# Phase D of a two-layer decoder: five hand-written engine orders in rounds of slots, with tanh, exponential, sums and moments as pieces of their own

## Chip, cores, metric

One core of one Trainium2 chip. The metric is the device time in microseconds of one launch, the median of the runs. The engines are TensorE (PE), VectorE (DVE), ScalarE (ACT), GpSimd (POOL) and SyncE (SP), which issues most DMAs; each runs its own list of instructions in order, and they meet by semaphores.

## The reference, cut to what matters

A decoder of two layers works on x of 32 × 256 × 256. Each layer has attention, cross attention and a feed-forward part, each behind a layernorm. The change touches only the attention of layer 1, which attends over the batch: for each of the 256 positions its 32 items attend to one another.

```python
def _L1_attn_ref(x, Wq, Wk):
    q = jnp.einsum('sbd,ed->sbe', x, Wq)
    k = jnp.einsum('sbd,ed->sbe', x, Wk)
    scores = jnp.einsum('sbd,tbd->bst', q, k) / scale
    align = jax.nn.softmax(jnp.tanh(scores), axis=2)
    return jnp.einsum('bst,tbd->sbd', align, x)
...
x = x + _L0_ffn_ref(_layernorm(x), ...)
x = x + _L1_attn_ref(_layernorm(x), L1_attn_Wq, L1_attn_Wk)
x = x + _L1_xattn_ref(_layernorm(x), ctx_768, ...)
```

## The kernel before, in words

The kernel has four phases with a barrier of all engines after each: A (layer 0, both attentions and routing), C (the 16 experts), **D** (this attention) and E (the rest of layer 1). Phase D runs from about 1885 to 2062 us of the span.

Phase D has `STEPS_D` = 16 steps. One takes 16 positions of all 32 items, 512 rows of 256 numbers: four groups g of 128 rows (a group is 32 items times 4 positions). For step t:

- SP loads slots, rows and gates (`sp_d_load`, ring of 4), the first four steps in phase C, the others when the sum `x3` of the step four earlier is made.
- POOL gathers each row's expert answer by four indirect DMAs (`pool_d_gather`, L1952, ring of 2).
- DVE adds gate × answer + x into `x3` (L1963), takes statistics (L1968), aggregates (L1972), and adds epsilon to the variance (L1976). POOL raises that to the power −1/2 (L1982). DVE normalises into `xn` (L1990).
- PE turns `xn` in two halves (`pe_d_turn`, L2000); ACT copies each (L2010). PE projects in two halves with the joined weights (`pe_d_project`, L2018); ACT copies each (L2028). PE scores (`pe_d_score`, L2037), all four groups into one bank.
- ACT takes tanh (L2048) and exponential (L2050) of the 128 × 512 scores. DVE masks them, so that a row sees its own position only (L2057).
- PE sums, a group at a time, with a column of ones for the denominator (`pe_d_sum`, L2065), into banks 4 and 5 in turn: sum g waits until out g − 2 has read the bank. DVE takes the reciprocal (L2073) and writes the output rows (L2076). SP stores the step (L2083).

The trace has two records for each matmul of project, score and sum, and one for each of turn.

The order is written out by hand in a loop over rounds for each engine: in round t a piece with lag 3 works on step t − 3. PE: score and then turn, two sums, project, two sums, where turn and project have lag 3 and the others lag 4. DVE: mask (lag 4), add and moments (lag 2), outs 0 and 1 (lag 4), normalise (lag 2), outs 2 and 3 (lag 4). ACT: tanh and exponential (lag 4), both copies of turn, both of project (lag 3). POOL: gather (lag 1), power (lag 2). SP: load (lag 0), store (lag 4).

The other phases are written with a helper that puts each piece at a slot of a round:

```python
def due(n, period, slots, items=B):
    for k, slot in enumerate(slots):
        b, off = divmod(n - slot, period)
        if off == 0 and 0 <= b < items:
            yield b, k
```

The functions that the diff touches, with what calls them:

Of the kernel before, what the change touches and what calls it, by code (L numbers as in the profile page):

```python
# [12 lines left out]
ACT = mybir.ActivationFunctionType  # L13
# [110 lines left out]
def item(t, lag, n=B):  # L124
    return t - lag if 0 <= t - lag < n else None
# [1917 lines left out]
def act_d_exp(c, t):  # L2043
    s, par = c.sa.s, t % 2
    flat = c.sa.weight[par][:, :, :].rearrange("p g n -> p (g n)")
    c.act.wait_ge(s.scored, t + 1)
    c.act.wait_ge(s.summed, 4 * (t - 1))
    c.nc.scalar.activation(flat, c.banks[par][:, :], ACT.Tanh, scale=1.0 / math.sqrt(D)).then_inc(s.exp, 1)  # L2048
    c.act.wait_ge(s.exp, 2 * t + 1)
    c.nc.scalar.activation(flat, flat, ACT.Exp).then_inc(s.exp, 1)  # L2050


def dve_d_mask(c, t):

    s, r, par = c.sa.s, c.sa, t % 2
    c.dve.wait_ge(s.exp, 2 * t + 2)
    c.nc.vector.tensor_tensor(r.weight[par][:, :, :], r.weight[par][:, :, :],  # L2057
                              r.same[:, :].unsqueeze(1).broadcast_to([P, G, P]), ALU.mult).then_inc(s.weight, 1)


def pe_d_sum(c, t, g):
    s, r, bank = c.sa.s, c.sa, 4 + g % 2
    c.pe.wait_ge(s.weight, t + 1)
    c.pe.wait_ge(*c.bank_out[bank])
    c.nc.tensor.matmul(c.banks[bank][:, 0:D + 1], r.weight[t % 2][:, g, :], r.xn[t % 4][:, g, :], start=True,  # L2065
                       stop=True).then_inc(s.summed, 1)
    c.bank_out[bank] = (s.out, 4 * t + g + 1)
# [20 lines left out]
def pe_phase_d(c):  # L2090
    for t in range(LAST_D):
        t3, t4 = (item(t, lag, STEPS_D) for lag in (3, 4))
        if t4 is not None:
            pe_d_score(c, t4)
        if t3 is not None:
            for k in range(KC):
                pe_d_turn(c, t3, k)
        if t4 is not None:
            for g in range(2):
                pe_d_sum(c, t4, g)  # L2100
        if t3 is not None:
            for n in range(KC):
                pe_d_project(c, t3, n)
        if t4 is not None:
            for g in range(2, G):
                pe_d_sum(c, t4, g)


def act_phase_d(c):
    for t in range(LAST_D):  # L2110
        t3, t4 = (item(t, lag, STEPS_D) for lag in (3, 4))
        if t4 is not None:
            act_d_exp(c, t4)
        if t3 is not None:
            for k in range(KC):
                act_d_xn_t(c, t3, k)
            for n in range(KC):
                act_d_project(c, t3, n)


def dve_phase_d(c):
    for t in range(LAST_D):
        t2, t4 = (item(t, lag, STEPS_D) for lag in (2, 4))
        if t4 is not None:
            dve_d_mask(c, t4)
        if t2 is not None:
            dve_d_stats(c, t2)
        if t4 is not None:
            for g in range(2):
                dve_d_out(c, t4, g)  # L2130
        if t2 is not None:
            dve_d_normed(c, t2)
        if t4 is not None:
            for g in range(2, G):
                dve_d_out(c, t4, g)


def pool_phase_d(c, d):
    for t in range(LAST_D):
        t1, t2 = (item(t, lag, STEPS_D) for lag in (1, 2))  # L2140
        if t1 is not None:
            pool_d_gather(c, d["expert_out"], t1)
        if t2 is not None:
            pool_d_power(c, t2)


def sp_phase_d(c, d):
    out_rows = d["x4"].rearrange("b (t q g) d -> t b q g d", g=G, q=Q)
    for t in range(LAST_D):
        t0, t4 = (item(t, lag, STEPS_D) for lag in (0, 4))  # L2150
        if t0 is not None and t0 >= 4:
            sp_d_load(c, d, t0)
        if t4 is not None:
            sp_d_out(c, out_rows[t4], t4)
# [414 lines left out]
```

## Time and profile before

| | |
|---|---|
| median of 3 runs | 3380.1 us (3377.64 to 3380.84) |
| profiled execution | 3377.66 us, its span 3375.9 us |
| granted clock over the span | 0.972 of full speed |
| busy: PE, DVE, ACT, POOL | 92%, 69%, 53%, 38% |

The profile is of one execution. "PE L2018 ... x8" in its timeline is eight records on line 2018, run one after the other; "[1.20 <-DVE sa_p L2057]" says that the engine was idle for 1.20 us before, and what ended that. A group's length there counts to the end of its last record, and where records overlap, the next group starts before that end. The names of tiles are `sa_xn` (normalised rows), `sa_xnt` (turned), `sa_q` (projected), `sa_p` (weights), `sa_rec` (reciprocals), `sa_y` (gathered), `sa_g` (gates).

### The profile page before, as it was taken

To read this page: it belongs to the slowest core of one execution; us is meant where nothing else is said; L and a number is where in the kernel's file an instruction comes from. 1 tells how busy PE (TensorE), PEld (TensorE's weight loads), DVE (VectorE), ACT (ScalarE), POOL (GpSimd) and SP (SyncE) were. 2 spreads that over 40 slices of the span, in tenths; PEclk is the share of its full clock that TensorE was granted. 3 is DMA by queue.
4 is the path that set the end of the run, shared out by engine and by line. 5 is a ranking of instruction groups with operands and counts; after the bars stand their busy time and mean duration, and the time that the engine had idled before them with its cause. 6 is when DMAs were issued, how large, how long until landed. Compare 5 with 4: busy or idle time off the path is not lost. (4 is left out here: it accounts for less than half of the span.)

```text
span 3375.9 us, 57669 instructions
## 1 busy us (share of the span) xinstructions
PE 3101.4 (92%) x21302; PEld 2150.3 (64%) x21302; DVE 2328.1 (69%) x4781; ACT 1799.4 (53%) x3243; POOL 1295.6 (38%) x1933
## 2 busy tenths in 40 slices
PE   3899999999999998699999786899999999999997
PEld 2566666666666665466666453576766667666764
DVE  3588888888888887242111484687888877888774
ACT  3788788888788874211111132555555555555552
POOL 4366666666666663100000351233333333333322
PEclk8899999999999999799999897999999999999998
DMA  5877777878777873333333253433433434433420
GB/s 99 149 119 107 105 109 108 112 101 110 104 107 108 108 99 48 118 117 117 117 104 123 78 168 80 64 62 58 68 60 56 62 59 67 63 56 59 62 39 13
DMA packets 291102, 301.17 MB, mean 89 GB/s; under 512 B 35243, under 2 KB 278427, under 8 KB 290821
## 3 DMA queue, kind: packets, MB, share of 16 engines
q1 hardware_dynamic: 276420, 273.41, 48.4%
q0 software_dynamic: 6144, 15.68, 1.6%
q10 hardware_dynamic: 8256, 8.39, 0.8%
q8 instruction: 169, 2.77, 0.4%
q14 instruction: 113, 0.92, 0.1%
HBM read 95.51 MB, written 50.40 MB: 43 GB/s over the span
## 5 line engine op out<-in xcount | busy, mean ns | idle before, releaser
L493 DVE TENSOR_REDUCE xa_mx<-bank 128x2 f32<-128x512 f32 x1024 | 670.5, 688 | 151.8 <-PE bank L483 146.5
L597 ACT ACTIVATE xa_p<-bank 128x512 f32<-128x512 f32 x1024 | 568.5, 599 | 310.6 <-PE bank L587 305.4
L608 DVE SCALAR_TENSOR_TENSOR xa_p<-xa_p,bank 128x1024 f32<-128x1024 f32 x256 | 306.6, 1217 | 38.4 <-PE bank L576 23.4
L933 POOL TENSOR_SCALAR_AFFINE_SELECT xa_p<-xa_p 128x256 f32<-128x256 f32 x512 | 201.7, 406 | 222.1 <-ACT xa_p L924 209.8
L620 PE MATMUL bank<-xa_p,xa_v 128*32 128x256 f32 x4096 | 277.3, 389 | 1.7 <-DVE xa_p L608 1.4
L924 ACT ACTIVATE xa_p<-bank 128x384 f32<-128x384 f32 x512 | 236.9, 492 | 54.3 <-PE bank L912 36.0
L1952 POOL DMA_INDIRECT sa_y<-expert_out,sa_s x64 | 70.1, 1095 | 508.2 <-POOLq L1853 482.5
L1747 ACT ACTIVATE ex_h<-bank,ex_b 128x512 f32<-128x512 f32 x64 | 44.0, 687 | 361.7 <-PE bank L1736 361.7
L1736 PE MATMUL bank<-ex_xt,ex_w 128*128 128x512 f32 x512 | 224.6, 597 | 0.7 <-ACT ex_xt L1727 0.7
L1766 PE MATMUL bank<-ex_w,ex_h 128*128 128x256 f32 x1024 | 224.0, 379 | 1.0 <-issue 0.9
L587 PE MATMUL bank<-ex_w,xa_ks 99*128 99x256 bf16 x1024 | 183.9, 277 | 30.5 <-ACT xa_p L597 22.2
L1766 PEld LDWEIGHTS bank<-ex_w,ex_h 128*128 128x128 f32 x1024 | 193.4, 190 | 28.1 <-issue 2.4
L587 PE MATMUL bank<-xa_qs,xa_ks 99*128 99x256 bf16 x1024 | 185.2, 279 | 21.8 <-DMA xa_qs<-xa_row 16.2
L483 PE MATMUL bank<-xa_ks,ex_w 96*128 96x256 bf16 x1024 | 189.3, 276 | 16.3 <-DMA ex_w<-xa_pq 9.6
L483 PE MATMUL bank<-xa_ks,xa_qs 96*128 96x256 bf16 x1024 | 181.7, 274 | 5.8 <-DVE xa_mx L493 4.3
L1551 POOL TENSOR_TENSOR fp_v<-fp_v,fp_p 128x1408 f32<-128x1408 f32 x32 | 101.6, 3174 | 214.3 <-DVE fp_v L1542 214.3
L912 PE MATMUL bank<-ex_w 96*128 96x256 f16 (+1 forms) x1024 | 156.2, 250 | 21.4 <-DMA ex_w<-ra_parts 7.9
L2262 PE MATMUL bank<-ff_wg,fe_xnt 128*128 128x352 f32 x512 | 173.9, 463 | 0.9 <-ACT fe_xnt L2255 0.7
L454 PE MATMUL bank<-ff_wd,fe_ht 128*128 128x256 f32 x768 | 172.7, 382 | 0.7 <-ACT fe_ht L1651 0.7
L1736 PEld LDWEIGHTS bank<-ex_xt,ex_w 128*128 128x128 f32 x512 | 98.0, 192 | 118.0 <-issue 116.1
L620 PEld LDWEIGHTS bank<-xa_p,xa_v 128*32 128x32 f32 x4096 | 107.5, 109 | 99.1 <-issue 35.7
L1776 DVE TENSOR_TENSOR ex_y<-bank,ex_b 128x256 f32<-128x256 f32 x64 | 27.2, 425 | 203.6 <-PE bank L1766 203.6
(284 smaller groups left out, 6849.1 us busy)
## 6 DMA issues: line engine op xcount, KB each, us to landing
ex_w<-ra_parts SPq DMA_DIRECT2D x384, 128.0 KB, 6.6
xa_ks<-xa_pk SPq DMA_DIRECT2D x384, 128.0 KB, 4.6
ex_w<-in_L_ffn_W SPq DMA_DIRECT2D x32, 1024.0 KB, 7.2
xa_qs<-xa_pq SPq DMA_DIRECT2D x192, 128.0 KB, 4.7
ex_w<-xa_pq SPq DMA_DIRECT2D x192, 128.0 KB, 4.6
ra_x<-in_x SPq DMA_DIRECT2D x32, 256.0 KB, 8.1
xa_ctx<-in_ctx_t SPq DMA_DIRECT2D x64, 128.0 KB, 3.9
queue<-zeros ACTq DMA_DIRECT2D x4, 2048.0 KB, 7.9
```

What stands on the lines that cost most here:

```text
L454: m = c.nc.tensor.matmul(ps[:, tc * D:(tc + 1) * D], left[:, k, tc * P:(tc + 1) * P], right[:, k, :], start=(k == 0), stop=(k == chunks - 1))
L483: m = c.nc.tensor.matmul(ps[:, tc * S:(tc + 1) * S], c.xa.q_stack[par][0:STACK3, h, tc * P:(tc + 1) * P], c.xa.k_stack[par][0:STACK3, h, : ...
L493: c.nc.vector.tensor_reduce(c.xa.row_max[:, :, n], halves(c.banks[2 + n % 2]), AX.X, ALU.max).then_inc(s.max_taken, 1)
L587: m = c.nc.tensor.matmul(ps[:, kc * S:(kc + 1) * S], c.xa.k_stack[par][:, h, kc * P:(kc + 1) * P], c.xa.q_stack[par][:, h, :], start=True, ...
L597: c.nc.scalar.activation(c.xa.p_beside[:, n // 2 % 4, :, n % 2, :], halves(c.banks[n % 2]), ACT.Exp, scale=SCALE).then_inc(s.exp, 1)
L608: c.nc.vector.scalar_tensor_tensor(out=p, in0=p, scalar=1.0, in1=c.banks[bank][:, :].unsqueeze(1).broadcast_to([P, TC, 2 * S]), op0=ALU.mi ...
L620: m = c.nc.tensor.matmul(bank[WIDE * quad:WIDE * quad + WIDE, at + q0:at + S], v[:, kc, 4 * g + quad, :], p(4 * g + quad, kc), start=(kc = ...
L924: c.nc.scalar.activation(c.xa.p_after[:, n // 2 % 4, n % 2, 0:S + P], c.banks[n % 2][:, 0:S + P], ACT.Exp, scale=1.0 / math.sqrt(2.0 * DH) ...
L933: c.nc.gpsimd.affine_select(out=diagonal, in_=diagonal, compare_op=ALU.is_ge, fill=0.0, base=0, pattern=[[0, TC], [1, P]], channel_multipl ...
L1736: m = c.nc.tensor.matmul(c.banks[bank][:, :], r.w1[par][:, k, m1 * P:(m1 + 1) * P], r.x_t[par][:, k, :], start=(k == 0), stop=(k == KC - 1))
L1766: m = c.nc.tensor.matmul(c.banks[bank][:, 0:D], r.hid[par][:, k, q * P:(q + 1) * P], r.w2[par][:, k, :], start=(k == 0), stop=(k == MC - 1))
L2262: m = c.nc.tensor.matmul(c.banks[bank][:, 0:HALF], c.ff.xn_t[:, k, tc * P:(tc + 1) * P], w[:, k, cols], start=(k == 0), stop=(k == KC - 1))
```

## The change

All five order functions of phase D are written with `due`, each with a period for its engine and a slot for each piece. `act_d_exp` is cut into tanh and exponential with a semaphore each, and `dve_d_stats` into the addition and the moments; each of the four sums and outs has a slot of its own. The bank of the scores is now freed by the tanh's semaphore. The addition has one more wait, for the outs of the step four before. Line numbers in the changed kernel are larger by 7 to 18.

```diff
-    s.scored, s.exp, s.weight = c.sem("sa_score", n), c.sem("sa_exp", 2 * n), c.sem("sa_w", n)
+    s.scored, s.tanh, s.exp, s.weight = (c.sem("sa_" + name, n) for name in ("score", "tanh", "exp", "w"))
...
-def dve_d_stats(c, t):
+def dve_d_add(c, t):
...
     c.dve.wait_ge(s.y_in[par], 64 * (t // 2 + 1))
+    c.dve.wait_ge(s.out, 4 * (t - 3))
     for g in range(G):
         m = dve.scalar_tensor_tensor(out=r.x3[at][:, g, :], in0=r.y[par][:, g, :], scalar=r.gate[at][:, g:g + 1],
                                      in1=r.x[at][:, g, :], op0=ALU.mult, op1=ALU.add)
     m.then_inc(s.x3, 1)
+
+
+def dve_d_moments(c, t):
+    s, r, dve, at = c.sa.s, c.sa, c.nc.vector, t % 4
     c.dve.wait_ge(s.x3, t + 1)
...
-    c.bank_out[bank] = (s.exp, 2 * t + 1)
+    c.bank_out[bank] = (s.tanh, t + 1)
...
+def act_d_tanh(c, t):
     s, par = c.sa.s, t % 2
     c.act.wait_ge(s.scored, t + 1)
     c.act.wait_ge(s.summed, 4 * (t - 1))
-    c.nc.scalar.activation(flat, c.banks[par][:, :], ACT.Tanh, scale=1.0 / math.sqrt(D)).then_inc(s.exp, 1)
-    c.act.wait_ge(s.exp, 2 * t + 1)
-    c.nc.scalar.activation(flat, flat, ACT.Exp).then_inc(s.exp, 1)
+    c.nc.scalar.activation(flat_weight(c, t), c.banks[par][:, :], ACT.Tanh, scale=1.0 / math.sqrt(D)).then_inc(s.tanh, 1)
+
+
+def act_d_exp(c, t):
+    s = c.sa.s
+    c.act.wait_ge(s.tanh, t + 1)
+    c.nc.scalar.activation(flat_weight(c, t), flat_weight(c, t), ACT.Exp).then_inc(s.exp, 1)
...
-LAST_D = STEPS_D + 4
+ROUND_D = dict(pe=9, dve=8, act=6, pool=2, sp=2)
...
 def pe_phase_d(c):
-    for t in range(LAST_D):
...
+    period = ROUND_D["pe"]
+    for n in range((STEPS_D - 1) * period + 48):
+        for b, k in due(n, period, (27, 28), STEPS_D):
+            pe_d_turn(c, b, k)
...
+        for b, k in due(n, period, (41, 42, 44, 47), STEPS_D):
+            pe_d_sum(c, b, k)
```

PE's other slots are 30 and 31 for project and 34 for score. DVE: add 16, moments 18, normalise 20, mask 33, outs 35, 37, 38, 39. ACT: copies of turn 19, 20, copies of project 22, 23, tanh 24, exponential 27. POOL: gather 2, power 5. SP: load 0, store 9.

TensorE in a steady round, before. L2037 is score, L2000 turn, L2065 sum, L2018 project.

```order
L2037 MATMUL bank<-sa_q,sa_xnt 128x128 x8
L2000 MATMUL bank<-ident,sa_xn 128x128 x8
L2065 MATMUL bank<-sa_xn,sa_p 128x257 x2
L2018 MATMUL bank<-sa_xnt,sa_wqk 128x512 x4
L2065 MATMUL bank<-sa_xn,sa_p 128x257 x2
```

And in the changed kernel, from one turn to the next. L2048 is score, L2011 turn, L2083 sum, L2029 project.

```order
L2011 MATMUL bank<-ident,sa_xn 128x128 x8
L2083 MATMUL bank<-sa_xn,sa_p 128x257
L2029 MATMUL bank<-sa_xnt,sa_wqk 128x512 x4
L2083 MATMUL bank<-sa_xn,sa_p 128x257 x2
L2048 MATMUL bank<-sa_q,sa_xnt 128x128 x8
L2083 MATMUL bank<-sa_xn,sa_p 128x257
```

With turn of step u, the row before it is the third sum of u − 2, the one behind it the fourth of u − 2, the two behind project are the first two of u − 1. Before, all four sums of a step stood between its score and the next step's score, the first two behind the next turn; now a step's first sum stands behind the next step's project, and its fourth behind the turn of the step after.

VectorE in a steady round, before, from one mask on (L2057 mask, L1963 add, L1968, L1972 and L1976 moments, L2073 and L2076 outs, L1990 normalise; one more pair of out rows follows).

```order
L2057 TENSOR_TENSOR sa_p<-sa_p,sa_same 128x512
L1963 SCALAR_TENSOR_TENSOR sa_x<-sa_y,sa_g,sa_x 128x256 x4
L1968 BN_STATS sa_stats<-sa_x 128x6 x4
L1972 BN_AGGR sa_mv<-sa_stats 128x2 x4
L1976 TENSOR_SCALAR sa_var<-sa_mv 128x4
L2073 RECIPROCAL sa_rec<-bank 128x1
L2076 SCALAR_TENSOR_TENSOR sa_out<-bank,sa_rec,sa_x 128x256
L2073 RECIPROCAL sa_rec<-bank 128x1
L2076 SCALAR_TENSOR_TENSOR sa_out<-bank,sa_rec,sa_x 128x256
L1990 TENSOR_SCALAR sa_xn<-sa_x,sa_mv,sa_rstd 128x256 x4
L2073 RECIPROCAL sa_rec<-bank 128x1
L2076 SCALAR_TENSOR_TENSOR sa_out<-bank,sa_rec,sa_x 128x256
```

And in the changed kernel, from an add on (L1970 add, L2075 mask, L1979, L1983 and L1987 moments, L2091 and L2094 outs, L2001 normalise; two more pairs of out rows follow).

```order
L1970 SCALAR_TENSOR_TENSOR sa_x<-sa_y,sa_g,sa_x 128x256 x4
L2075 TENSOR_TENSOR sa_p<-sa_p,sa_same 128x512
L1979 BN_STATS sa_stats<-sa_x 128x6 x4
L1983 BN_AGGR sa_mv<-sa_stats 128x2 x4
L1987 TENSOR_SCALAR sa_var<-sa_mv 128x4
L2091 RECIPROCAL sa_rec<-bank 128x1
L2094 SCALAR_TENSOR_TENSOR sa_out<-bank,sa_rec,sa_x 128x256
L2001 TENSOR_SCALAR sa_xn<-sa_x,sa_mv,sa_rstd 128x256 x4
L2091 RECIPROCAL sa_rec<-bank 128x1
L2094 SCALAR_TENSOR_TENSOR sa_out<-bank,sa_rec,sa_x 128x256
```

The add now stands before the mask, one out instead of two between the variance and normalise, and three outs instead of two behind normalise. ScalarE takes the exponential of a step behind the copies of the next step's turn, no longer right behind its tanh. The rows of POOL and SP stand in the order they had.

## Rows read from the trace of the kernel before

**Rows 1.** The page's part 1: busy time, share of the span, instructions, engine by engine

```profile
PE 3101.4 (92%) x21302; PEld 2150.3 (64%) x21302; DVE 2328.1 (69%) x4781; ACT 1799.4 (53%) x3243; POOL 1295.6 (38%) x1933
```

**Rows 2.** Waits from 1909 to 2058: engine, line, waited for: us in total, times, longest

```profile
PE bank L2065 <- DVE sa_p L2057: 20.1, 16, 2.1
```

**Rows 3.** Stretches: us, busy us of each engine, granted clock, DMA share, GB/s

```profile
1937.07:2040.27 103.20, 89.99 (x442) 61.08 (x440) 86.08 (x287) 37.27 (x67) 56.06 (x51) 1.00 0.48 154
2070.00:2100.00 30.00, 16.76 (x56) 9.81 (x57) 10.82 (x23) 4.17 (x7) 4.77 (x5) 0.65 0.55 81
```

**Rows 4.** Timeline of a steady round: start us, us, engine, line, operation, idle before

```profile
1922.07 1.06 ACT L2010 ACTIVATE sa_xnt<-bank 128x512 f32<-128x512 f32 x2
1922.19 0.69 DVE L2057 TENSOR_TENSOR sa_p<-sa_p,sa_same 128x512 f32<-128x512 f32 x1 [1.26 <-ACT sa_p L2050]
...
1922.94 1.14 PE L2065 MATMUL bank<-sa_xn,sa_p 128*128 128x257 f32 x4 [1.20 <-DVE sa_p L2057]
...
1923.91 3.60 PE L2018 MATMUL bank<-sa_xnt,sa_wqk 128*128 128x512 f32 x8
...
1926.36 0.17 DVE L1976 TENSOR_SCALAR sa_var<-sa_mv 128x4 f32<-128x4 f32 x1
...
1926.62 1.04 POOL L1982 TENSOR_TENSOR sa_rstd<-sa_var,mhalf 128x4 f32<-128x4 f32 x1 [2.86 <-DVE sa_var L1976]
...
1927.35 1.12 PE L2065 MATMUL bank<-sa_xn,sa_p 128*128 128x257 f32 x4
1927.55 0.60 ACT L2028 ACTIVATE sa_q<-bank 128x512 f32<-128x512 f32 x1 [1.12 <-PE bank L2018]
1927.69 1.38 DVE L1990 TENSOR_SCALAR sa_xn<-sa_x,sa_mv,sa_rstd 128x256 f32<-128x256 f32 x4
...
1928.31 1.95 PE L2037 MATMUL bank<-sa_q,sa_xnt 128*128 128x128 f32 x16
...
1928.99 0.16 DVE L2073 RECIPROCAL sa_rec<-bank 128x1 f32<-128x1 f32 x1
...
1929.59 0.16 DVE L2073 RECIPROCAL sa_rec<-bank 128x1 f32<-128x1 f32 x1
...
1930.09 1.04 PE L2000 MATMUL bank<-ident,sa_xn 128*128 128x128 f32 x8
...
1930.92 0.63 ACT L2050 ACTIVATE sa_p<-sa_p 128x512 f32<-128x512 f32 x1
```

**Rows 5.** Timeline: normalise and turn of step 0, score of step 0, normalise of step 2

```profile
1897.90 1.44 DVE L1990 TENSOR_SCALAR sa_xn<-sa_x,sa_mv,sa_rstd 128x256 f32<-128x256 f32 x4 [1.17 <-POOL sa_rstd L1982]
...
1899.40 1.97 PE L2000 MATMUL bank<-ident,sa_xn 128*128 128x128 f32 x8 [17.81 <-DVE sa_xn L1990]
...
1909.43 2.05 PE L2037 MATMUL bank<-sa_q,sa_xnt 128*128 128x128 f32 x16 [0.69 <-ACT sa_q L2028]
...
1918.31 1.44 DVE L1990 TENSOR_SCALAR sa_xn<-sa_x,sa_mv,sa_rstd 128x256 f32<-128x256 f32 x4
```

**Rows 6.** Timeline of the phase's end: the last four sums, reciprocals and outs

```profile
2054.33 3.59 PE L2065 MATMUL bank<-sa_xn,sa_p 128*128 128x257 f32 x8 [2.07 <-DVE sa_p L2057]
2055.09 0.17 DVE L2073 RECIPROCAL sa_rec<-bank 128x1 f32<-128x1 f32 x1 [0.81 <-PE bank L2065]
...
2058.15 0.48 DVE L2076 SCALAR_TENSOR_TENSOR sa_out<-bank,sa_rec,sa_x 128x256 f32<-128x256 f32 x1
```

**Rows 7.** Timeline of GpSimd's gathers and SP's store in steady rounds

```profile
1940.79 1.01 POOL L1952 DMA_INDIRECT sa_y<-expert_out,sa_s  x1 [0.31 <-issue]
1942.10 1.22 POOL L1952 DMA_INDIRECT sa_y<-expert_out,sa_s  x1 [0.30 <-issue]
...
1958.44 0.56 SPq L2083 DMA_DIRECT2D x<-sa_out  x1
...
1966.94 1.07 POOL L1952 DMA_INDIRECT sa_y<-expert_out,sa_s  x1 [1.74 <-DMA sa_g<-gates]
```

**Rows 8.** DMA issues from 1885 to 2062: count, median us from issue to landing

```profile
sa_y<-expert_out,sa_s POOLq DMA_INDIRECT x64, 3.2
```

More of the change, by code:

```diff
@@ L1944, in sp_d_first, with sp_d_next @@
         sp_d_load(c, d, t)
+def sp_d_next(c, d, t):
+    if t >= 4:
+        sp_d_load(c, d, t)
 def pool_d_gather(c, answer, t):
@@ L2039, in pe_d_score, with flat_weight @@
     m.then_inc(s.scored, 1)
-    c.bank_out[bank] = (s.exp, 2 * t + 1)
-def act_d_exp(c, t):
+    c.bank_out[bank] = (s.tanh, t + 1)
+def flat_weight(c, t):
+    return c.sa.weight[t % 2][:, :, :].rearrange("p g n -> p (g n)")
+def act_d_tanh(c, t):
     s, par = c.sa.s, t % 2
-    flat = c.sa.weight[par][:, :, :].rearrange("p g n -> p (g n)")
     c.act.wait_ge(s.scored, t + 1)
     c.act.wait_ge(s.summed, 4 * (t - 1))
-    c.nc.scalar.activation(flat, c.banks[par][:, :], ACT.Tanh, scale=1.0 / math.sqrt(D)).then_inc(s.exp, 1)
-    c.act.wait_ge(s.exp, 2 * t + 1)
-    c.nc.scalar.activation(flat, flat, ACT.Exp).then_inc(s.exp, 1)
+    c.nc.scalar.activation(flat_weight(c, t), c.banks[par][:, :], ACT.Tanh, scale=1.0 / math.sqrt(D)).then_inc(s.tanh, 1)
[3 more added lines that the diff above has]
+    c.nc.scalar.activation(flat_weight(c, t), flat_weight(c, t), ACT.Exp).then_inc(s.exp, 1)
 def dve_d_mask(c, t):
     s, r, par = c.sa.s, c.sa, t % 2
-    c.dve.wait_ge(s.exp, 2 * t + 2)
+    c.dve.wait_ge(s.exp, t + 1)
     c.nc.vector.tensor_tensor(r.weight[par][:, :, :], r.weight[par][:, :, :],
@@ L2083, in sp_d_out @@
     c.nc.sync.dma_start(rows, c.sa.out[par][:, :, :]).then_inc(s.out_there[par], 16)
-LAST_D = STEPS_D + 4
+ROUND_D = dict(pe=9, dve=8, act=6, pool=2, sp=2)
 def pe_phase_d(c):
-    for t in range(LAST_D):
[L2092 to L2106, printed above, removed]
@@ L2109, in act_phase_d @@
-def act_phase_d(c):
[L2110 to L2135, printed above, removed]
@@ L2138, in pool_phase_d @@
-def pool_phase_d(c, d):
[L2139 to L2144, printed above, removed]
+    period = ROUND_D["pe"]
+    for n in range((STEPS_D - 1) * period + 48):
+        for b, k in due(n, period, (27, 28), STEPS_D):
+            pe_d_turn(c, b, k)
+        for b, k in due(n, period, (30, 31), STEPS_D):
+            pe_d_project(c, b, k)
+        for b, _ in due(n, period, (34,), STEPS_D):
+            pe_d_score(c, b)
+        for b, k in due(n, period, (41, 42, 44, 47), STEPS_D):
+            pe_d_sum(c, b, k)
@@ new lines, in dve_phase_d @@
+def dve_phase_d(c):
+    period = ROUND_D["dve"]
+    for n in range((STEPS_D - 1) * period + 40):
+        for b, _ in due(n, period, (16,), STEPS_D):
+            dve_d_add(c, b)
+        for b, _ in due(n, period, (18,), STEPS_D):
+            dve_d_moments(c, b)
+        for b, _ in due(n, period, (20,), STEPS_D):
+            dve_d_normed(c, b)
+        for b, _ in due(n, period, (33,), STEPS_D):
+            dve_d_mask(c, b)
+        for b, k in due(n, period, (35, 37, 38, 39), STEPS_D):
+            dve_d_out(c, b, k)
@@ new lines, in act_phase_d @@
+def act_phase_d(c):
+    period = ROUND_D["act"]
+    for n in range((STEPS_D - 1) * period + 28):
+        for b, k in due(n, period, (19, 20), STEPS_D):
+            act_d_xn_t(c, b, k)
+        for b, k in due(n, period, (22, 23), STEPS_D):
+            act_d_project(c, b, k)
+        for b, _ in due(n, period, (24,), STEPS_D):
+            act_d_tanh(c, b)
+        for b, _ in due(n, period, (27,), STEPS_D):
+            act_d_exp(c, b)
+def pool_phase_d(c, d):
+    period = ROUND_D["pool"]
+    for n in range((STEPS_D - 1) * period + 6):
+        for b, _ in due(n, period, (2,), STEPS_D):
+            pool_d_gather(c, d["expert_out"], b)
+        for b, _ in due(n, period, (5,), STEPS_D):
+            pool_d_power(c, b)
@@ L2147, in sp_phase_d @@
 def sp_phase_d(c, d):
     out_rows = d["x4"].rearrange("b (t q g) d -> t b q g d", g=G, q=Q)
[L2149 to L2154, printed above, removed]
+    period = ROUND_D["sp"]
+    for n in range((STEPS_D - 1) * period + 10):
+        for b, _ in due(n, period, (0,), STEPS_D):
+            sp_d_next(c, d, b)
+        for b, _ in due(n, period, (9,), STEPS_D):
+            sp_d_out(c, out_rows[b], b)
```

## The prediction

> **What bounds the kernel now.** I read the page's busy line first: TensorE is busy for 92% of the span [rows 1], so the span moves only with what TensorE does or waits for. The change touches phase D alone, so the second view is the list of waits over that phase. It shows one wait of weight on TensorE: 16 times, 20.1 us in all, and at most 2.1, for the masked weights of VectorE before the first sum of a round [rows 2]. The third view is the table of stretches. The stretch from 1937.07 to 2040.27 runs from the start of normalise(4) to that of normalise(15), 11 rounds in 103.20 us: **9.38 us a round**, in which PE is busy for 89.99 / 11 = 8.18 and VectorE for 86.08 / 11 = 7.83, at a granted clock of 1.00 [rows 3]. The fourth is the timeline of one round [rows 4]. PE runs score, turn, a wait of 1.20, two sums, project, two sums, and starts the next score. The wait is a chain: score's last product, tanh, exponential, mask. Nothing stands between turn and sum to cover it. Normalise(2) starts at 1918.31 [rows 5], 18.76 or two more rounds ahead of that stretch: 13 rounds in all.
>
> So a perfect order could save 9.38 − 8.18 = 1.20 us a round, some 16 us of the run. The question is whether this one does.
>
> **The change part by part.** I write u for the step that VectorE normalises, and count from the start of normalise(u), called 0.
>
> *No operation is added or removed.* Tanh, exponential, sums and moments are the same instructions, some with another semaphore. VectorE's new wait in the addition, for the outs of step u − 4, is met: those ran on the same engine a round and more earlier. I cost it at nothing. What counts is the order.
>
> *TensorE* now has turn(u), the last sum of u − 2, project(u), two sums of u − 1, score(u), and the third sum of u − 1. Masked weights are asked for after project, not after turn. Mask(u − 1) ends at about 6.3 (add at 3.9, mask 1.7 later, 0.69 long), while the first sum comes at 1.47 + 1.04 + 0.76 + 3.44 = 6.7: the start of turn, turn's length, sum and gap up to project, and project from 1923.91 to the next sum at 1927.35 [rows 4]. The old wait of 1.20 is gone. In its place come two.
>
> First, project(u) waits for both copies of turn(u), since only one sum lies between. Turn's first half takes 0.66 (estimate: half of turn's 1.04 to its fourth start, and 0.27 for the product); the two copies take 1.06 [rows 4]. Project can start about 1.8 after turn does, and turn and a sum (half of the 0.96 between the sums at 1927.35 and the score at 1928.31) fill 1.52. That leaves 0.3 us idle. Score is not delayed: its queries are copied by 1928.15, in 4.24 from project's start, and project with two sums takes 3.44 + 0.96 = 4.40.
>
> Second, turn(u + 1) waits for normalise(u + 1), so VectorE's round has to be worked out.
>
> *VectorE* now has normalise(u), outs 1, 2 and 3 of u − 2, add(u + 1), mask(u − 1), moments(u + 1), out 0 of u − 1, normalise(u + 1). Step by step:
>
> - Turn(u) starts 1.44 to 1.50 after normalise does: 1897.90 to 1899.40 [rows 5], or a normalise of 1.38 with the same 0.06 [rows 4]. I take 1.47.
> - The last sum of u − 2 stands behind turn(u), 1.04 later: 2.51. The reciprocal follows a sum's start by 0.76 [rows 6], so out 3 starts at 3.27. VectorE would have reached it at 1.30 + 2 × 0.60 = 2.50 (normalise's 1.30 to the next reciprocal, outs 0.60 apart [rows 4]). It waits 0.8 us. This wait is new.
> - Out 3: 0.60, to 3.87. Add, mask, statistics and aggregation are the four groups that took from 1922.19 to 1926.36, 4.17 [rows 4]: the variance starts at 8.04. Exponential(u − 1) stands behind the copies of turn(u), which end at 1.47 + 0.66 + 1.06 = 3.2, and takes 0.63 [rows 4]: done near 3.9, before the mask at 5.6.
> - From variance to normalise it was 1.33 (1926.36 to 1927.69), through GpSimd's power of 1.04. Before, two outs filled this; now one does (its sum started at 6.7, ready at 7.5), and some 0.65 is idle. Normalise(u + 1) starts at 8.04 + 1.33 = 9.37.
>
> The new round is **9.37 us against 9.38**. TensorE's 1.20 has turned into 0.3 before project and 0.9 before turn; VectorE has exchanged 1.3 before the mask for 0.8 before out 3 and 0.65 before normalise. With the two ends of turn's start the round is 9.34 to 9.40, over 13 rounds −0.5 to +0.3 us. A step's error of 0.1 us would be 1.3 us.
>
> *Loads and gathers.* The order on SP's and GpSimd's queues is as before, but each still starts from out 3. SP stores, then loads; the gather waits for the gates. Storing began at 1958.44 and the gather at 1966.94: 8.50, the longest of the waits in this phase [rows 7]. Four gathers take 3 × 1.31 + 1.22 = 5.15 [rows 7], power 1.04. The loop through them spans two rounds: 3.98 to the store, + 8.50 + 5.15 + 1.04 + 0.03 = 18.70, or 9.35 a round. That is under 9.37, so hidden, but by almost nothing; with the other, shorter landings it has more room. The last gather is issued at 3.98 + 8.50 + 3 × 1.31 = 16.4 and lands 3.2 later [rows 8], near 19.6; add(u + 3) needs it at 2 × 9.37 + 3.87 = 22.6, so gathered data are no limit.
>
> *Filling.* Score(0) starts at 1909.43 as before [rows 5], and turn(1) 1.78 later at 1911.21 (1928.31 to 1930.09 [rows 4]). Copies end near 1913.2, project(1) runs 1913.3 to 1916.7 without waiting for the mask, the reciprocal of the first sum is at 1917.45, and normalise(2) starts at 1918.05 instead of 1918.31: −0.3 us.
>
> *Draining.* Step 15 is normalised at N = 1918.05 + 13 × 9.37 = 2039.86. Its score starts at N + 7.7, tanh, exponential and mask take it to N + 11.1, but VectorE still has outs 2 and 3 of step 14, whose sums run behind score: to N + 11.4. From the first of the last four sums to the last out's end it was 2054.33 to 2058.63, 4.30 [rows 6], and a mask starts 0.75 before its sum (1922.19 to 1922.94 [rows 4]), together 5.05. So VectorE ends at N + 16.5 = 2056.4 instead of 2058.63: **−2.2 us**, which already contains the gains of filling and of the round.
>
> *Behind the phase.* The next phase starts 2.2 us earlier and is untouched. Its first stretch runs with a granted clock of 0.65 [rows 3], between the levels of 1.2 and 2.4 GHz; when the clock returns may shift a little. I take 0, and as bounds ±3 us, the spread of the runs shown.
>
> **Sum.** 3377.66 − 2.2 = 3375.5 for the profiled execution. That execution lay 2.4 us below the median of the runs, 3380.1, so the median becomes 3377.9. About 0.2%, 6.8 us, is what a measurement of this kernel can tell from no change; the forecast is inside.
>
> **The rivals.**
>
> *TensorE's round, faster.* If out 3 did not wait for turn, VectorE would need 9.37 − 0.77 = 8.60 a round, and TensorE 8.18 + 0.3 = 8.5. Price: 13 × 0.78 = 10.1 us and the 2 of the ends: 3368. For it speaks that both engines are busy for only 7.8 and 8.2 of 9.38 [rows 3]. Against it: the last sum stands in TensorE's row behind a turn that waits for the normalisation in front of the out, with no other route. Chance 0.06.
>
> *The gates' loop, slower.* Store, load, gather, power becomes the longest ring. It decides when landing and gather take longer than 8.54 + 5.15 in most rounds. Slower by over 6.8 us needs rounds of 10.05, a loop of 20.1, 1.4 us longer than the longest seen. With landings 2 us longer the round is 10.35: +12.7 − 2 = +10.7, 3391. For it speaks the thin margin of 0.02 a round; against it, 8.50 was the longest and in most rounds it was less, and the transfers are as many and as close together as before. A gather issue took 1.22 in place of 1.01 as the fourth of its group, beside add and statistics [rows 7]; four of 1.22 add 0.6 to the loop and make the round 9.7, or +2 us in all. The Trainium skill (GPSIMD Engine Reference, Specifications) has GpSimd's SBUF interfaces shared with VectorE, with contention when a VectorE instruction has two SBUF inputs or a two-port mode; adds and masks have two. By that rule alone the loop is that much longer wherever the gather meets them, which is the start of this rival and is not enough for it. Chance 0.04.
>
> *The chip does what is written but the change gives nothing at all*, not even the ends: 3380, inside the forecast's own case.
>
> **How the numbers follow.** No measurable change 0.90, faster 0.06, slower 0.04. The range, 3373.0 to 3382.5, takes in 2.2 us from the ends or none, ±1.3 for the round, ±3 behind the phase; the rivals lie outside it and hold 0.1.
>
> **What would show it.** Normalise starts 9.3 to 9.45 us apart; VectorE waits 0.8 for TensorE's last sum before a reciprocal and some 0.6 for the power; TensorE's wait for the mask is gone, with about 0.9 before turn for the normalisation and 0.3 before project for ScalarE; the last out of phase D ends 2 us earlier. Rounds under 9.0 or over 9.8 us would make it wrong, and so would a wait of VectorE for gathered rows.

## The result, and the profile after

The changed kernel took **3369.24 us in the median of 12 runs, against 3377.76 for 12 runs of the kernel before** beside it. The ratio is 0.9981, with a 95% interval of 0.9974 to 0.9989. Two later comparisons on other occasions gave 0.9981 (0.9972 to 0.9990) and 0.9985 (0.9976 to 0.9994). So the change is faster, by 0.15 to 0.19% or some 6 us. That is clear of no change and just inside the 0.2% that I had set as the bound. The two medians of the first comparison lie 8.5 us apart, which is more than its ratio says (6.4 us); I go by the ratio and its interval. The forecast of 3377.9 and its range, 3373.0 to 3382.5, were wrong: the median lies 3.8 us below the range.

The profiled execution alone would have hidden this. It took 3377.60 us, as long as that of before (3377.66). From VectorE's first memset of phase D to its memset in phase E, phase D took 171.84 us in it, against 176.64. The rest, which the change does not touch, was 1.2 us longer ahead of phase D and 3.5 us longer behind it. So for the phase I read the trace, and for the kernel the comparison of many runs.

Over 13 steady rounds, from normalise(2) to normalise(15), the view of stretches has 120.46 us in place of 121.96. Columns are as in [rows 3].

```profile
1919.01:2039.47 120.46, 109.92 (x530) 71.31 (x530) 101.77 (x340) 44.20 (x78) 66.24 (x61) 1.00 0.50 158
```

The waits have changed hands. Columns as in [rows 2]:

```profile
POOL sa_y L1958 <- DMA sa_g<-gates: 27.4, 11, 3.8
...
DVE sa_xn L2001 <- POOL sa_rstd L1993: 9.9, 13, 1.9
...
PE bank L2011 <- DVE sa_xn L2001: 6.8, 13, 1.8
DVE sa_p L2075 <- ACT sa_p L2068: 5.6, 1, 5.6
...
PE bank L2083 <- DVE sa_p L2075: 1.5, 1, 1.5
```

TensorE's wait for the mask was 16 times and 20.1 us [rows 2]. It has come down to one, at the end of the phase. In its place are 13 waits for the normalised rows, together only 6.8 us, and VectorE waits 9.9 us for the power. And GpSimd waits 11 times and 27.4 us for the gates, with 3.8 the longest, where it was 7 times and 8.6 us before; I had expected that to stay hidden.

One undisturbed round, normalise(12) to normalise(13), in order of time, answers to [rows 4] (the view ends soon after 2021.35, so it has one of the four groups of the last normalise):

```profile
2012.38 1.39 DVE L2001 TENSOR_SCALAR sa_xn<-sa_x,sa_mv,sa_rstd 128x256 f32<-128x256 f32 x4 [0.57 <-POOL sa_rstd L1993]
...
2013.82 1.09 PE L2011 MATMUL bank<-ident,sa_xn 128*128 128x128 f32 x8 [0.26 <-DVE sa_xn L2001]
...
2014.51 1.09 ACT L2021 ACTIVATE sa_xnt<-bank 128x512 f32<-128x512 f32 x2 [0.76 <-PE bank L2011]
...
2014.75 0.60 PE L2083 MATMUL bank<-sa_xn,sa_p 128*128 128x257 f32 x2
...
2015.39 0.17 DVE L2091 RECIPROCAL sa_rec<-bank 128x1 f32<-128x1 f32 x1 [0.43 <-PE bank L2083]
...
2015.65 3.70 PE L2029 MATMUL bank<-sa_xnt,sa_wqk 128*128 128x512 f32 x8 [0.30 <-issue]
2015.99 1.67 DVE L1970 SCALAR_TENSOR_TENSOR sa_x<-sa_y,sa_g,sa_x 128x256 f32<-128x256 f32 x4
...
2017.58 0.68 DVE L2075 TENSOR_TENSOR sa_p<-sa_p,sa_same 128x512 f32<-128x512 f32 x1
...
2019.19 1.03 PE L2083 MATMUL bank<-sa_xn,sa_p 128*128 128x257 f32 x4
...
2020.02 0.17 DVE L1987 TENSOR_SCALAR sa_var<-sa_mv 128x4 f32<-128x4 f32 x1
...
2020.28 1.04 POOL L1993 TENSOR_TENSOR sa_rstd<-sa_var,mhalf 128x4 f32<-128x4 f32 x1 [1.13 <-DVE sa_var L1987]
...
2021.35 0.41 DVE L2001 TENSOR_SCALAR sa_xn<-sa_x,sa_mv,sa_rstd 128x256 f32<-128x256 f32 x1 [0.57 <-POOL sa_rstd L1993]
```

Normalise to normalise is 8.97 us, not 9.37. The order of waits is as predicted. TensorE is idle 0.26 us before turn, for the normalised rows, where I had expected 0.9, and 0.30 before project; VectorE waits 0.43 for the last sum before out 3, and 0.57 for the power. The sizes were not as predicted.

Four of the 13 rounds were 8.96 to 8.98 and the last 8.93; the others were 9.19 to 9.49, and one 10.46. That one shows the second loop, in the views of SP, GpSimd and VectorE:

```profile
1987.69 0.56 SPq L2101 DMA_DIRECT2D x<-sa_out  x1
...
1996.69 1.29 POOL L1958 DMA_INDIRECT sa_y<-expert_out,sa_s  x1 [3.77 <-DMA sa_g<-gates]
...
2001.32 1.00 POOL L1958 DMA_INDIRECT sa_y<-expert_out,sa_s  x1 [0.30 <-issue]
2002.33 1.05 POOL L1993 TENSOR_TENSOR sa_rstd<-sa_var,mhalf 128x4 f32<-128x4 f32 x1
...
2000.59 0.40 DVE L1987 TENSOR_SCALAR sa_var<-sa_mv 128x4 f32<-128x4 f32 x1
...
2003.41 0.74 DVE L2001 TENSOR_SCALAR sa_xn<-sa_x,sa_mv,sa_rstd 128x256 f32<-128x256 f32 x2 [1.89 <-POOL sa_rstd L1993]
```

The store was issued at 1987.69, and the gather could start at 1996.69, 9.00 us later. The last of its four issues ended at 2002.32. The power stood behind it, though its variance had been started at 2000.59; normalise(11) came at 2003.41 in place of 2001.92.

The end of the phase answers to [rows 6]. The last sums of the kernel before run from 2054.33 to 2057.92. First a stretch of the kernel before, within its last sums, with the granted clock as the third number from the end:

```profile
2055.00:2057.00 2.00, 2.00 (x6) 1.00 (x5) 1.30 (x4) 0.00 (x0) 0.00 (x0) 0.50 0.00 0
```

Then a stretch of the changed kernel within its last sums, and its timeline from the last mask on:

```profile
2052.00:2055.00 3.00, 2.02 (x8) 0.88 (x6) 2.34 (x8) 0.00 (x0) 0.00 (x0) 1.00 0.42 175
...
2050.85 0.68 DVE L2075 TENSOR_TENSOR sa_p<-sa_p,sa_same 128x512 f32<-128x512 f32 x1
...
2051.58 1.14 PE L2083 MATMUL bank<-sa_xn,sa_p 128*128 128x257 f32 x4 [1.54 <-DVE sa_p L2075]
2052.32 0.17 DVE L2091 RECIPROCAL sa_rec<-bank 128x1 f32<-128x1 f32 x1 [0.79 <-PE bank L2083]
...
2054.60 0.48 DVE L2094 SCALAR_TENSOR_TENSOR sa_out<-bank,sa_rec,sa_x 128x256 f32<-128x256 f32 x1
```

From the last mask to the end of the last out it is 2050.85 to 2055.08, 4.23 us; before it was 5.05. In the kernel before, the granted clock fell to 0.50, the level of 1.2 GHz, at 2054.88, when the first of the four sums had been issued; now it is 1.00, 2.4 GHz, through all four. The wait ahead of them was 2.07 before and is 1.54 now. A shorter wait alone does not keep the clock up: in the run "Out 1 into the wait for the power" below it was 1.54 too, and the clock fell in the middle of the last sums.

### The profile page after: what moved, and what is told of

Read it like the earlier page. It is cut to its first block and busy times, and to the rows that moved or that the text cites. A ratio compares the mean times of both kernels' runs of the same rounds, so it can differ in the third digit from the quotient of the medians.

```text
span 3375.8 us, 57669 instructions
## 1 busy us (share of the span) xinstructions
PE 3106.5 (92%) x21302; PEld 2149.3 (64%) x21302; DVE 2325.9 (69%) x4781; ACT 1800.6 (53%) x3243; POOL 1295.6 (38%) x1933
## 3 DMA queue, kind: packets, MB, share of 16 engines
q10 hardware_dynamic: 8256, 8.39, 0.8%
```

## The experiments

All lengths of phase D here are from VectorE's first memset of the phase to its memset in the next. "Ratio" is to the kernel before.

### The changed kernel again

> The changed kernel once more, for its time and a second profile. Two theories of the first result. Theory A (two loops): the loop normalise, turn, fourth sum, out 3, add, mask, moments, power gives 8.97 us a round, and a second loop of two rounds through store, load of the gates, gather and power adds to some rounds, 0.3 us on average in the first profile. Then single rounds of 8.97 appear again between longer ones, the longer ones are those in which GpSimd's power starts right behind its gather, phase D (from VectorE's memset at its start to the memset of the next phase) is 169 to 173 us against 176.6 before, and the time is 5 to 8 us below before. Theory B (ends only): rounds are 9.3 to 9.4 on average whatever the profile, and the time is 2 to 4 us below before.

Measured: 3365.36 against 3372.01, ratio 0.9981 (0.9972 to 0.9990). Phase D took 169.61 us. Its 13 rounds were 9.40, then six of 8.96 or 8.97 (and a last of 8.93) mixed with five of 9.17 to 9.20, 118.1 in all. Theory A holds and B falls: the gain is not at the ends alone. One point of A was too simple. In the five longer rounds the power did not queue behind the gather. The variance ahead of it took 0.38 to 0.40 us in place of 0.17 and ended with the gather's last issue (see the last section).

### The load ahead of the store

```diff
-    for n in range((STEPS_D - 1) * period + 10):
+    for n in range((STEPS_D - 1) * period + 14):
...
-        for b, _ in due(n, period, (9,), STEPS_D):
+        for b, _ in due(n, period, (11,), STEPS_D):
             sp_d_out(c, out_rows[b], b)
```

> The changed kernel with one slot changed: SP issues the load of a step ahead of the store that it stood behind (store at slot 11 in place of 9). Theory A: the loads no longer hang on out 3, GpSimd's wait for the gates is nearly gone, every steady round is 8.95 to 9.0 us, phase D 167 to 168.5 us, and the time 3 to 4 us below the changed kernel's. Theory C (the long rounds come from something else, such as transfers that slow VectorE or late gathered rows): rounds stay uneven with a mean near 9.3 and the time does not move.

Measured: 3364.98 us, beside 3365.36 for the changed kernel, ratio 0.9981 (0.9972 to 0.9990). Phase D 169.10 us; after a first round of 9.41 all were 9.01 to 9.03, and 8.93 the last. GpSimd's wait for the gates is gone, and it waits 2.5 us for the variance in each round:

```profile
1949.12 1.04 POOL L1993 TENSOR_TENSOR sa_rstd<-sa_var,mhalf 128x4 f32<-128x4 f32 x1 [2.54 <-DVE sa_var L1987]
1950.35 1.19 POOL L1958 DMA_INDIRECT sa_y<-expert_out,sa_s  x1 [0.19 <-issue]
...
1954.45 1.14 POOL L1958 DMA_INDIRECT sa_y<-expert_out,sa_s  x1 [0.30 <-issue]
1958.14 1.04 POOL L1993 TENSOR_TENSOR sa_rstd<-sa_var,mhalf 128x4 f32<-128x4 f32 x1 [2.54 <-DVE sa_var L1987]
```

The loop through the gates is gone, as A said, and with it all uneven rounds. But three of A's numbers missed: the rounds (8.95 to 9.0), the phase (167 to 168.5) and the gain in time, which was not 3 to 4 us but none that these runs show. The changed kernel beside it had a phase of 169.6, so only 0.5 us was left to gain. And each round is 0.05 longer than the undisturbed 8.97. That stands in one place: turn starts 1.49 to 1.50 after normalise here, and 1.44 there. The gather's first issue, 1.19 long, now runs beside normalise. That the loop costs a time that differs between executions is part of the finding: against this run, 2.7 us in the first profile, 0.5 and 1.0 in the two others, by the phase's length.

### The same edit on the kernel before

```diff
-    for t in range(LAST_D):
-        t0, t4 = (item(t, lag, STEPS_D) for lag in (0, 4))
+    for t in range(LAST_D + 1):
+        t0, t4 = (item(t, lag, STEPS_D) for lag in (0, 5))
```

> The kernel before with the same edit on SP alone. Theory A: its rounds were set by TensorE waiting for the mask, 9.38 us, and the gates' loop was hidden, so rounds stay 9.37 to 9.39, phase D 176 to 177 us, the time within 0.1% of before; GpSimd's wait for the gates of 8.6 us disappears without effect. Theory C (store and load collide, and their order matters in itself): the time moves by 2 us or more.

Measured: 3370.53 against 3372.01, ratio 0.9996 (0.9987 to 1.0005). Phase D 176.61 us, rounds 9.38 to 9.39. The gates' wait had cost the kernel before nothing, and theory C falls. Its round was set by the wait for the mask, which is unchanged; columns and stretch as in [rows 2]. The phase ran 5 us later in this execution, so that the stretch ends before the sixteenth wait, of 2.1 us:

```profile
DVE sa_p L2057 <- ACT sa_p L2050: 24.4, 15, 6.4
...
PE bank L2065 <- DVE sa_p L2057: 18.0, 15, 1.2
```

### Out 1 into the wait for the power

```diff
-        for b, k in due(n, period, (35, 37, 38, 39), STEPS_D):
+        for b, k in due(n, period, (35, 35, 38, 39), STEPS_D):
             dve_d_out(c, b, k)
```

> The changed kernel with out 1 moved from behind normalise to ahead of it (slot 35), where it fills VectorE's wait for the power. Theory A (a loop of waits, not a sum of idle times): VectorE's wait for the power shrinks by up to 0.6 us and its wait for the fourth sum grows from 0.43 to about 1.0; the round without the gates' loop stays 8.95 to 9.05 and the time within 1.5 us of the changed kernel. Theory D (VectorE's idle time is what counts): the round falls by 0.5 to 0.6, and the time by 6 to 8 us.

Measured: 3365.24 us, ratio 0.9978 (0.9969 to 0.9987), beside 0.9981 for the changed kernel. Phase D 171.56 us. Undisturbed rounds 8.95 to 8.97, four of 9.19 or 9.20 and one of 10.45. The timeline shows VectorE's idle time moved from one place to the other:

```profile
1966.91 0.17 DVE L1987 TENSOR_SCALAR sa_var<-sa_mv 128x4 f32<-128x4 f32 x1
...
1967.78 0.48 DVE L2094 SCALAR_TENSOR_TENSOR sa_out<-bank,sa_rec,sa_x 128x256 f32<-128x256 f32 x1
1968.24 1.38 DVE L2001 TENSOR_SCALAR sa_xn<-sa_x,sa_mv,sa_rstd 128x256 f32<-128x256 f32 x4
...
1969.73 0.48 DVE L2094 SCALAR_TENSOR_TENSOR sa_out<-bank,sa_rec,sa_x 128x256 f32<-128x256 f32 x1
1971.24 0.17 DVE L2091 RECIPROCAL sa_rec<-bank 128x1 f32<-128x1 f32 x1 [1.03 <-PE bank L2083]
```

Nothing is idle before normalise any more, and the wait before out 3 has grown from 0.43 to 1.03. The sum of both is the same, as theory A had it. D is refuted: idle time inside a loop is what is left over from the loop's length, and work moved into it buys nothing.

This profile also shows what the clock costs at the phase's end. The last sums start at 2045.01, again after a wait of 1.54, and the granted clock falls to 0.50 at 2046.91, within the third sum. From the first sum to the last out's end it is 4.02 us, against 3.50 in all three profiles of the changed kernel.

### TensorE's order undone

```diff
+        for b, k in due(n, period, (38, 38, 41, 42), STEPS_D):
+            pe_d_sum(c, b, k)
         for b, _ in due(n, period, (34,), STEPS_D):
             pe_d_score(c, b)
-        for b, k in due(n, period, (41, 42, 44, 47), STEPS_D):
-            pe_d_sum(c, b, k)
```

> The changed kernel with TensorE's order alone undone: the first two sums of a step stand behind the next turn again, the other two behind project. Theory A (loops of waits, worked out with the durations of the changed kernel's trace): the sums behind turn now wait for a mask that VectorE takes after three outs and an addition, and the fourth sum for an out behind normalise, so a round is 11.0 to 11.4 us, phase D some 195 us, the time 25 us above the changed kernel's. Theory E (the gain comes from the orders of VectorE and ScalarE): a round stays at 9.0 to 9.4.

Measured: 3400.0 us in two runs, ratio 1.0066 (1.0048 to 1.0084). Phase D 196.88 us, rounds 10.45 to 10.5 and two of 11.9. The wait for the mask is back:

```profile
PE bank L2083 <- DVE sa_p L2075: 22.3, 11, 2.0
...
DVE sa_p L2075 <- ACT sa_p L2068: 17.8, 11, 1.6
```

So the new rows of VectorE and ScalarE are not what gains; with TensorE's old row they cost 20 us. They only pay with a row that asks for the mask behind project. Theory E falls. The round was 0.6 us shorter than A had worked out, the phase as long. The two rounds of 11.9 stand beside stretches of 3.4 us, from 1919.64 and from 1964.02, with a granted clock of 0.50, and are 2.9 us longer together than two others; the phase's end is 4.4 us longer than in the kernel before.

### Two sums under the copies of turn

```diff
-        for b, k in due(n, period, (41, 42, 44, 47), STEPS_D):
+        for b, k in due(n, period, (41, 42, 47, 47), STEPS_D):
             pe_d_sum(c, b, k)
```

with the load ahead of the store, as above.

> The changed kernel with the load ahead of the store, and the third sum moved from ahead of the next turn to behind it, beside the fourth. TensorE now has two sums under the copies of turn and no wait before project. Theory A: VectorE's loop gets longer, since outs 2 and 3 both stand behind turn: 1.44 + 0.93 + 0.63 to out 2, 1.2 for both outs, 4.03 for add, mask and moments, 1.33 for the power: 9.55 us a round, phase D 175 to 176 us, slower than the changed kernel by 4 to 8 us. Theory F (TensorE's own row sets the round): 8.3 to 8.7.

Measured: 3379.23 against 3379.14, ratio 1.0002 (0.9992 to 1.0013). Phase D 176.48 us, rounds of 9.61 to 9.64 and 9.52 the last, where theory A had 9.55. VectorE now waits at out 2, for the sum that has moved behind turn:

```profile
1951.61 1.44 DVE L2001 TENSOR_SCALAR sa_xn<-sa_x,sa_mv,sa_rstd 128x256 f32<-128x256 f32 x4 [0.57 <-POOL sa_rstd L1993]
...
1953.15 0.48 DVE L2094 SCALAR_TENSOR_TENSOR sa_out<-bank,sa_rec,sa_x 128x256 f32<-128x256 f32 x1
1954.66 0.17 DVE L2091 RECIPROCAL sa_rec<-bank 128x1 f32<-128x1 f32 x1 [1.03 <-PE bank L2083]
```

TensorE has no wait before project, and the kernel is no faster than before. Theory F falls.

### The balanced rows

TensorE as in the last kernel and the load ahead of the store, and VectorE:

```diff
-    for n in range((STEPS_D - 1) * period + 40):
+    for n in range((STEPS_D - 1) * period + 44):
...
-        for b, _ in due(n, period, (20,), STEPS_D):
+        for b, _ in due(n, period, (21,), STEPS_D):
             dve_d_normed(c, b)
-        for b, _ in due(n, period, (33,), STEPS_D):
+        for b, _ in due(n, period, (34,), STEPS_D):
             dve_d_mask(c, b)
-        for b, k in due(n, period, (35, 37, 38, 39), STEPS_D):
+        for b, k in due(n, period, (36, 38, 43, 43), STEPS_D):
             dve_d_out(c, b, k)
```

VectorE's row is then normalise, out 1, add, moments, mask, outs 2 and 3, out 0. Behind normalise it has work for the whole time until turn and two sums are through, and behind the variance for the whole time of the power.

> As sums_behind_turn, and VectorE's row in another order: normalise, out 1, add, moments, mask, outs 2 and 3, out 0, so that nothing of it stands waiting for turn. Theory A: VectorE needs 7.9 to 8.1 a round, TensorE 8.2 with no wait left, so a round is 8.2 to 8.35 us, phase D 159 to 162 us, and the time 14 to 16 us below before, 0.42 to 0.48%. If TensorE still waits in each round, the name of what ends the wait tells which size is wrong.

Measured: 3364.65 against 3379.14, ratio **0.9962** (0.9949 to 0.9976). Phase D 161.06 us, rounds 8.38 or 8.39, three of 8.26 to 8.28. TensorE has no wait left; from the view of stretches:

```profile
1920.00:2030.00 110.00, 110.00 (x534) 72.58 (x534) 103.35 (x343) 43.36 (x79) 64.43 (x57) 1.00 0.51 164
```

It is busy for all of the 110 us, and this phase is now bound by its products. What is left over stands on VectorE, which waits 0.26 us a round for the sum ahead of out 0.

> The balanced kernel once more, on one chip with the changed kernel. By the phase in the profiles (161.1 us against 169.6 to 171.8) it should be 8 to 11 us below the changed kernel and 14 to 16 us below before; the rounds 8.3 to 8.4 us again, all alike. If the time lay within 3 us of the changed kernel, the gain of the phase would be lost in the next one.

Measured: 3363.13 against 3375.53, ratio 0.9964 (0.9951 to 0.9978), phase D 162.00 us, rounds as before with one of 9.14. The changed kernel on the same chip had 3368.43:

> The changed kernel beside it. Theory A: 5 to 8 us below before; rounds of 8.97 and longer ones mixed, phase D 169 to 172 us, its last four sums at a granted clock of 1.00 and 15.6 us from the last normalise to the last out. If the long rounds were an accident of the first profiles, all would be 8.97 here.

ratio 0.9985 (0.9976 to 0.9994), phase D 170.10 us, seven undisturbed rounds of 8.93 to 8.97, the others 9.19 to 9.55. So the balanced kernel is 5.3 us below the changed kernel by the medians, some 7 by the ratios, and 8.1 by the phase. It beats both kernels, by less than I expected (8 to 11 us below the changed kernel, 14 to 16 below before). The interval of its ratio is 0.27% wide, 9 us, so whether part of the phase's gain is lost behind it stays open.

### The store ahead of the load in the balanced kernel

```diff
-        for b, _ in due(n, period, (11,), STEPS_D):
+        for b, _ in due(n, period, (9,), STEPS_D):
             sp_d_out(c, out_rows[b], b)
```

> As balanced, but with SP's store ahead of the load, as in the changed kernel. Out 3 now comes late in VectorE's round, and the loop out 3, store, load of the gates, gather, power spans two rounds. Theory A: 7.3 to out 3, 0.7 to the store, 8.1 to the gates' landing, 5.2 for the gathers and 1.1 for the power are 22.4, so a round is 10.9 to 11.4 us, phase D 193 to 200 us, the time 30 to 38 us above balanced. Theory C (the gates do not hold anything up): as balanced.

Measured: 3396.29 us in two runs, ratio 1.0055 (1.0037 to 1.0073). Phase D 190.31 us, the 11 rounds between the first (8.26) and the last (9.33) are 10.0 to 12.2, on average 10.98; the time is 32 us above balanced. Rounds and time are as theory A had them, the phase is 3 us shorter, and C falls. GpSimd's wait for the gates is the largest of all:

```profile
POOL sa_y L1958 <- DMA sa_g<-gates: 48.0, 10, 7.0
...
DVE sa_xn L2001 <- POOL sa_rstd L1993: 17.0, 8, 3.8
PE bank L2011 <- DVE sa_xn L2001: 15.7, 8, 3.7
```

In all these 11 rounds GpSimd's power starts 0.02 to 0.03 us behind the end of the gather's last issue: the loop closes in each. One slot in SP's row is worth 29 us of the phase here, and 0.5 to 3 in the changed kernel. Not all of the 29 is the loop's own length: with TensorE's longer waits the mean granted clock from 1920 to 2040 is 0.93, where it is 1.00 in balanced, and this run can't separate the two. The loop store, load, gates, gather, power is shown by taking it away and by making it longer.

## Why the prediction was wrong

The mechanism was right and the sizes were not. The step that failed is VectorE's loop, put at 9.37 us a round where it took 8.97; a second one is the end of the phase, put at 5.05 us where it took 4.23. Three terms, with what three profiles of the changed kernel measured:

| | predicted | first | again | third |
|---|---|---|---|---|
| filling, memset to normalise(2) | −0.3 | −0.5 | −0.4 | −0.6 |
| 13 rounds | −0.1 | −1.5 | −3.9 | −3.2 |
| draining, normalise(15) to phase E | −1.8 | −2.8 | −2.8 | −2.7 |
| phase D | −2.2 | −4.8 | −7.0 | −6.5 |

**The round, 9.37 against 8.97.** The sum's steps were in the right order: TensorE's two new waits, VectorE's two, and the loop through them came as written. Four sizes were wrong, all too long, and they add up to the 0.40:

- "The last sum of u − 2 stands behind turn(u), 1.04 later." It was 0.93 (2013.82 to 2014.75). 1.04 was the length of turn's row before a wait, which includes the tail of its last product; the next start comes before that.
- "The reciprocal follows a sum's start by 0.76." It was 0.64 (2014.75 to 2015.39). I took it from the first sum behind a wait, at the phase's end [rows 6]. A sum behind a turn is faster; behind a wait it is 0.74 in the changed kernel as well (2051.58 to 2052.32).
- "Add, mask, statistics and aggregation … 4.17." It was 4.03 (2015.99 to 2020.02). In the old order the statistics stood right behind the additions whose result they need; in the new one the mask stands between. From the first addition to the next instruction it is 1.59 here (2015.99 to 2017.58) and was 1.70 with the statistics next (1922.80 to 1924.50, below). The balanced kernel has the statistics there again, and 1.70 again in every round.
- Turn started 1.44 after normalise, not 1.47.

```profile
1922.80 1.67 DVE L1963 SCALAR_TENSOR_TENSOR sa_x<-sa_y,sa_g,sa_x 128x256 f32<-128x256 f32 x4
...
1924.50 1.41 DVE L1968 BATCH_NORM_STATS2 sa_stats<-sa_x 128x6 f32<-128x256 f32 x4
```

The range had room for one step's error of 0.1, 1.3 us over 13 rounds. But four steps were taken from rows with other neighbours, all four came out too long, and together that is 5.2 us. The stated ends of the range, 3373.0 and 3382.5, are not even the sum of its terms, which is 3373.6 to 3384.4; the result lies below either.

**The loop of the gates** was named as the slower rival, with a chance of 0.04. It "decides when landing and gather take longer than 8.54 + 5.15", 13.69 together. With two rounds of 8.97, the store at 3.72 and 1.07 for the power, the bound is 17.94 − 3.72 − 1.07 = 13.15. From a store's issue to the end of the gather's last issue it took 12.0 to 14.6 us in the three profiles; the longest is the one shown, 1987.69 to 2002.32. That sum tells the long rounds from the short ones, in the 11 rounds from normalise(4) to normalise(14) of each profile:

- In the 17 rounds longer than 9.1 it was 13.28 or more. In four of them the power queued behind the gather (9.47 to 9.55 us). In twelve the variance was held to the gather's end (9.17 to 9.20). The round of 10.46 had both.
- In 15 of the other 16 it was 12.9 or less. In the last it was 13.5, right behind the round of 10.46, which had given it room.

So this loop took back 0.5 to 3 us, in a kernel that was faster all the same. I had priced this rival against my round only, and not against a faster one. And I had put the longest landing beside the gathers of another round: in the kernel before, landing and gathers of one round took up to 13.84 (1958.44 to 1972.28), over 13.69 in four of 11.

**Draining.** The last mask was where I put it, 11.4 after normalise(15): 2050.85 − 2039.47 = 11.38. What followed took 4.23 and not 5.05. I had carried over the row of before, in which the sums from the second on ran at 1.2 GHz; in the new order all run at 2.4. This is 0.8 of the missing 0.9 us, the rest is rounding in my sum.

**The faster rival** did not occur: out 3 still waits for turn, at 0.43 us in place of my 0.8. The rounds lie between my forecast and that rival's 8.60. That the median, 3369.24, is within 1.3 us of the rival's 3368 is chance. The signs to look for were rounds "under 9.0 or over 9.8 us": the undisturbed ones are 8.97, one was 10.46, and both count against the forecast.

**Behind the phase** I took 0 with ±3 us. The first profile had +3.5, and the median shows no effect of that kind: 0.19% is 6.4 us, the phase's gain in three profiles is 6.1 on average.

**The base.** The forecast was laid on 3380.1, the median of three runs of the kernel before. Its median over 12 runs is 3377.76. So 2.3 of the 8.7 us between forecast and result belong to the base and not to the change; laid on 3377.76 the forecast would have been 3375.6, still 6.3 us too high.

## What to carry to other kernels

Write the round as loops through engines and queues, and take for each step the distance from start to start in a row with the same neighbour in front; the length of a row that ends in a wait, or at another clock, is a different number. Give the round the error of all its steps, with one sign, times the number of rounds. Take the pieces of a loop from one and the same round, and test every slower loop against the faster round too, since what is hidden behind 9.4 us is not hidden behind 9.0. Idle time in a loop cannot be filled to gain anything; the loop has to be cut, here by giving VectorE other work behind normalise and SP the load ahead of the store.

## What I had not expected of the hardware

A small instruction of VectorE can be held up while GpSimd issues an indirect DMA. The variance (128 × 4) takes 0.17 us alone. In 13 rounds of the changed kernel's three profiles an issue of the gather had started 0.58 us earlier (the last of its four, and the third in the round of 10.46); the variance took 0.38 to 0.41, and normalise came 1.55 after it in place of 1.33 (2.82 in the round of 10.46). The round of normalise(12) shown above is one without it: the variance at 2020.02 takes 0.17, the power starts at 2020.28 and normalise at 2021.35. A round with it, VectorE and GpSimd:

```profile
1952.46 1.42 POOL L1958 DMA_INDIRECT sa_y<-expert_out,sa_s  x1 [0.30 <-issue]
...
1954.19 1.00 POOL L1958 DMA_INDIRECT sa_y<-expert_out,sa_s  x1 [0.30 <-issue]
...
1954.77 0.39 DVE L1987 TENSOR_SCALAR sa_var<-sa_mv 128x4 f32<-128x4 f32 x1
...
1955.24 1.04 POOL L1993 TENSOR_TENSOR sa_rstd<-sa_var,mhalf 128x4 f32<-128x4 f32 x1
1956.32 1.06 DVE L2001 TENSOR_SCALAR sa_xn<-sa_x,sa_mv,sa_rstd 128x256 f32<-128x256 f32 x3 [0.62 <-POOL sa_rstd L1993]
```

The power is not queued here: the gather's last issue starts at 1954.19 and ends at 1955.19, and the power follows the variance's end, 1955.16, as closely as ever. The difference of 0.22 us is that of the rounds of 9.19 and 8.97. The variance ends 0.03 before the issue in all 13 (the profile's ends on GpSimd are rough, but these agree). In four other rounds the issue had started only 0.2 to 0.3 us before the variance, which then took 0.17, while the power had to queue behind the issue. So a variance that starts late in an issue is held until the issue's end, and one that starts early is not. What in the issue holds it these rows do not tell, and no run was made for it. The Trainium skill (GPSIMD Engine Reference, Specifications) says that GpSimd shares its SBUF interfaces with VectorE, with contention when a VectorE instruction is in a two-port mode or has two SBUF inputs. The rows agree that the two engines hold each other up, VectorE too and not GpSimd alone; whether the variance, with one SBUF tensor for input, ran in such a mode they do not show. In my sum I had used that rule only for the gather's length. A gather issue that met the statistics took 1.42 us in place of 1.00 (at 1952.46 in the same profile).
